# Gates by DMA through DRAM, gate product on GpSimd, activation in PSUM, head reordered, in a recurrence and mixture-of-experts kernel

## Chip, cores and metric

The kernel runs on one core of one Trainium2 chip. The metric is the device time of one execution in microseconds (us), lower is better. Timelines below count from the first instruction of the profiled execution.

## What is computed

A tanh recurrence over 32 time steps gives `h`, with 32 sequences and 128 features. Then `h` is normalised (root mean square), a router picks 4 of 16 experts for each of the 1024 tokens, and all 16 experts are computed densely and summed with their gates, which are zero for those not picked. The result is `x + h + t`.

```python
xw = einsum('ntd,dh->nth', x, Wx) + b
h_t = tanh(xw_t + h_{t-1} @ Wh)                       # 32 steps, h_0 = cond
xn = h * rsqrt(mean(h * h, -1) + 1e-5) * norm_scale
logits = xn @ wg + bg
vals, idx = top_k(logits, 4);  gates = softmax(vals)  # gate_full: (1024, 16)
u = einsum('th,ehd->etd', xn, w1) + b1
a = minimum(u[..., ::2], 7.0);  b = clip(u[..., 1::2], -7.0, 7.0)
s = a * sigmoid(1.702 * a) * (b + 1.0)
y = einsum('eti,eih->eth', s, w2) + b2
out = x + h + einsum('eth,te->th', y, gate_full)
```

All arrays are float32.

## The kernel before

Tokens are laid out in 8 tiles of 128 columns (4 time steps of 32 sequences). Features stand on the partitions, tokens in the free dimension. The engines' programs are written out by hand: each engine runs its own list in order, with semaphores between them.

**Head** (L851 to L893 on TensorE). `keep_warm` issues bf16 matmuls on zeros. Tile 0 of `x` is transposed, `x_wx` multiplies by `Wx`, and `step(t)` (L763) adds `h @ Wh`; ScalarE's `tanh` (L403) makes the next `h`. The head has 8 steps (`HEAD`), with transposes of the other `x` tiles, the transpose of `b1`, sums of squares, `lay_rstd` and fillers between them. Then follow the statistics of the first 2 tiles, `normalise` on VectorE, and the router for them (`route_...`, `gates_...`).

**Unit loop** (L894). A unit is 512 columns wide. There are three stages (`CHUNKS` 2, 2 and 4 tiles): in the first two a unit is two experts by 256 tokens, in the third one expert by 512 tokens; 8, 8 and 16 units, 32 in all (`NU`). For unit `v`:

- TensorE: `up(v, 0)` into psA and `up(v, 1)` into psB (L808), three passes each with rounded high and low parts (float32r); `lay_gates(v - 1)` (L822), which multiplies a selection matrix by the transposed gates `gT`, so that every partition of psG holds the expert's gates; one recurrence step in each of the two slots up to step 31 (`steps_at`); `down(v - LAG)` (L838) in float32, which adds the expert's output to psY. On the way: `sums` and `raw_logits` (at `STATS`), `lay_rstd` (`RSTD`), `transpose_gates` (`GATES_T`), `transpose_out` (`ROWS_OUT`).
- ScalarE: `relu_a` from psA (L458), `swish` from it (L466), the tanh of the steps; before the loop all `w1_high` (L411), which round `w1`.
- VectorE: `lin` from psB (L685), `actg = act * psG` of the unit before (L703), `act` from `lin` and `swish` (L716), the lower parts of `w1` (`w1_low`, L603), `normalise`, and the router's small operations.
- GpSimd: powers (`rstd`, `expo`), `w1_low` for the second half of `w1` (L365), `xn_low`, `place_expo`, and `xh = xT + h` (`add_residuals`).
- SP issues all loads but `wh`, which is on GpSimd's queue, and the stores of each stage's rows.

The bank psM is shared: `psM_turn` fixes an order in which statistics, `rstd`, gates and output transposes take it, each waiting until the one before has been read.

After the last unit: `yT` (L731), four transposes (L937), two copies (L473, L733) and four stores.

## Time and profile before

| | |
|---|---|
| median of 3 runs | 128.18 us (126.57 to 128.47) |
| profiled execution, its time | 127.02 us |
| profiled execution, span from first to last instruction | 124.7 us |
| TensorE busy | 111.3 us, 89% |
| VectorE busy | 89.8 us, 72% |
| ScalarE busy | 65.4 us, 52% |
| GpSimd busy | 24.0 us, 19% |
| mean granted clock of TensorE | 0.999 |

Busy time is a share of the span. Ends of matmuls are modelled and matmuls overlap, so the distance between starts tells more than the lengths. In a timeline row, what stands in brackets is the idle time of the engine before the row and what ended it; `x2` at a float32 matmul counts the two records that one instruction leaves. A row's line number is that of the kernel's source.

### The profile page before, as it was taken

What the parts mean: (1) busy time and instruction counts of PE and PEld (TensorE: products, weight loads), DVE (VectorE), ACT (ScalarE), POOL (GpSimd) and SP (SyncE); (2) the same over time, 40 slices, a digit from 0 to 9 for tenths busy, and PEclk for the clock granted to TensorE, in tenths of its full rate; (3) what the DMA queues carried; (4) which work ended last, traced back from release to release, by engine and by line L of the source; (5) the groups of instructions that cost most, each with busy time, mean ns of one, the idle gap of its engine ahead of it and who ended that gap; (6) DMA issues with size and microseconds to landing.
All of it is one profiled execution on the core that took longest, in us unless ns stands there. A gap on an engine that the chain in (4) does not pass through costs nothing. (4 is left out here: it accounts for less than half of the span.)

```text
span 124.7 us, 1891 instructions
## 1 busy us (share of the span) xinstructions
PE 111.3 (89%) x611; PEld 91.6 (73%) x611; DVE 89.8 (72%) x238; ACT 65.4 (52%) x141; POOL 24.0 (19%) x44
## 2 busy tenths in 40 slices
PE   3669989979999999999999399999999999999850
PEld 2558779969989999899988398877766776677310
DVE  0105659899748999769977779897678877887830
ACT  4014593657663567566756166644665466546210
POOL 5200212940004066206401513000000000000000
PEclk9999999999999999999999999999999999999999
DMA  2899900000000000000000010000001000000003
GB/s 59 178 324 323 334 27 5 0 0 3 0 3 0 5 0 0 0 0 5 0 0 0 3 42 5 0 0 0 0 13 29 0 0 0 8 0 0 0 0 84
DMA packets 6189, 4.52 MB, mean 36 GB/s; under 512 B 754, under 2 KB 6100, under 8 KB 6148
## 3 DMA queue, kind: packets, MB, share of 16 engines
q1 hardware_dynamic: 6148, 4.34, 12.3%
q8 instruction: 5, 0.08, 0.3%
q0 software_dynamic: 32, 0.07, 0.2%
q14 instruction: 4, 0.03, 0.1%
HBM read 3.88 MB, written 0.52 MB: 35 GB/s over the span
## 5 line engine op out<-in xcount | busy, mean ns | idle before, releaser
L458 ACT ACTIVATE relu_a<-psA,lim_b1a 128x256 f32<-128x256 f32 (+1 forms) x48 | 25.8, 546 | 30.4 <-PE psA L808 30.4
L685 DVE TENSOR_SCALAR lin<-psB,one_b1b 128x256 f32<-128x256 f32 (+1 forms) x48 | 26.0, 569 | 16.5 <-PE psB L808 16.2
L838 PE MATMUL psY<-actg,w_sb 128*128 128x256 f32 (+1 forms) x96 | 33.6, 459 | 0.4 <-DVE actg L703 0.3
L808 PE MATMUL psA<-xn_hi,w_hi 128*128 128x256 f32 (+1 forms) x48 | 23.7, 495 | 0.0
L466 ACT ACTIVATE swish<-relu_a,limit_col 128x512 f32<-128x512 f32 x32 | 23.1, 722 | 1.0
L716 DVE SCALAR_TENSOR_TENSOR act<-lin,swish 128x512 f32<-128x512 f32 x32 | 22.3, 695 | 0.0
L703 DVE TENSOR_TENSOR actg<-act,psG 128x512 f32<-128x512 f32 x31 | 21.0, 678 | 0.0
L838 PEld LDWEIGHTS psY<-actg,w_sb 128*128 128x128 f32 x96 | 16.9, 189 | 4.1 <-DVE actg L703 1.9
L808 PE MATMUL psB<-xn_hi,w_hi 128*128 128x256 f32 (+1 forms) x48 | 16.7, 347 | 0.0
L808 PE MATMUL psA<-xn_hi,w_lo 128*128 128x256 f32 (+1 forms) x48 | 15.8, 330 | 0.0
L808 PE MATMUL psA<-xn_lo,w_hi 128*128 128x256 f32 (+1 forms) x48 | 15.8, 330 | 0.0
L808 PE MATMUL psB<-xn_lo,w_hi 128*128 128x256 f32 (+1 forms) x48 | 15.6, 325 | 0.0
L808 PE MATMUL psB<-xn_hi,w_lo 128*128 128x256 f32 (+1 forms) x48 | 15.6, 324 | 0.0
L822 PE MATMUL psG<-gT,select 128*128 128x256 f32 (+1 forms) x47 | 12.4, 320 | 0.8 <-DVE gT L597 0.8
L808 PEld LDWEIGHTS psA<-xn_hi,w_lo 128*128 128x128 f32 x48 | 9.7, 202 | 3.2 <-issue 2.9
L808 PEld LDWEIGHTS psA<-xn_hi,w_hi 128*128 128x128 f32 x48 | 9.6, 201 | 3.2 <-issue 2.9
L763 PEld LDWEIGHTS psR<-hT,wh_sb 128*128 128x128 f32 x56 | 10.0, 218 | 1.1 <-ACT hT L403 0.5
L763 PE MATMUL psR<-hT,wh_sb 128*128 128x32 f32 x56 | 10.1, 265 | 0.3 <-ACT hT L403 0.3
L403 ACT ACTIVATE hT<-psR,b_col 128x32 f32<-128x32 f32 x28 | 7.8, 279 | 4.7 <-PE psR L763 4.5
L808 PEld LDWEIGHTS psA<-xn_lo,w_hi 128*128 128x128 f32 x48 | 9.6, 200 | 0.7
L808 PEld LDWEIGHTS psB<-xn_hi,w_lo 128*128 128x128 f32 x48 | 9.4, 195 | 0.7
L808 PEld LDWEIGHTS psB<-xn_hi,w_hi 128*128 128x128 f32 x48 | 9.4, 195 | 0.7
(105 smaller groups left out, 131.4 us busy)
## 6 DMA issues: line engine op xcount, KB each, us to landing
w_sb<-in_L_ffn_w SPq DMA_DIRECT2D x4, 512.0 KB, 6.7
w_sb<-in_L_ffn_w SPq DMA_DIRECT2D x4, 256.0 KB, 7.2
x_sb<-in_x SPq DMA_DIRECT2D x1, 448.0 KB, 4.7
out<-y_sb SPq DMA_DIRECT2D x8, 32.0 KB, 1.6
out<-y_sb SPq DMA_DIRECT2D x4, 64.0 KB, 1.7
x_sb<-in_x SPq DMA_DIRECT2D x1, 64.0 KB, 2.1
wh_sb<-in_L_cond_Wh POOLq DMA_DIRECT2D x1, 64.0 KB, 2.4
wx_sb<-in_L_cond_Wx SPq DMA_DIRECT2D x1, 64.0 KB, 2.2
```

The costliest lines, as they stand in the source:

```text
L403: nc.scalar.activation(hT[:, (t + 1) * N:(t + 2) * N], step_psum(t), ACT.Tanh, bias=b_col[:, 0:1]).then_inc(step_done, 1)
L458: last = nc.scalar.activation(relu_a[:, u % 2, o], psA[u % 2][:, o], ACT.Relu, scale=-1.0, bias=lim_b1a[:, e0 + k:e0 + k + 1])
L466: nc.scalar.activation(swish[:, u % 3, 0:w], relu_a[:, u % 2, 0:w], ACT.Gelu_apprx_sigmoid, scale=-1.0, bias=limit_col[:, :]).then_inc(swi ...
L685: last = nc.vector.tensor_scalar(lin[:, v % 2, o], psB[v % 2][:, o], one_b1b[:, e0 + k:e0 + k + 1], LIMIT + 1.0, ALU.add, ALU.min)
L703: nc.vector.tensor_tensor(actg[:, u % SUM_DEPTH, o], act[:, u % 2, o], gate_bank(u)[:, o], ALU.mult).then_inc(actg_done, 1)
L716: nc.vector.scalar_tensor_tensor(act[:, v % 2, 0:w], lin[:, v % 2, 0:w], 1.0 - LIMIT, swish[:, v % 3, 0:w], ALU.max, ALU.mult).then_inc(ac ...
L763: nc.tensor.matmul(step_psum(t), wh_sb[:, :], hT[:, t * N:(t + 1) * N], start=False, stop=True, skip_group_check=True).then_inc(step_mm, 1)
L808: last = nc.tensor.matmul(o, w[:, e0 + k, a, :], x_part[:, cols(c)], start=(m == 0), stop=(m == 2))
L822: last = nc.tensor.matmul(gate_bank(u)[:, k * n:(k + 1) * n], select[:, e0 + k, :], gT[:, cols(c)], start=True, stop=True)
L838: last = nc.tensor.matmul(psY[:, 0:n], w2_sb[:, e0 + k, :], actg[:, u % SUM_DEPTH, part(c, k)], start=False, stop=(e0 + k == E - 1))
```

## The change

- `gT` is now 16 rows only. SP writes each pair of tiles' gates to a DRAM scratch (`gate_rows`) and reads it back with a source that repeats for all partitions into `gate_cols`, in four DMAs of four experts each (512 KB a DMA), each with its own semaphore. The matmuls of `lay_gates`, the selection matrix and the split of the gates into high and low parts go.
- The product `actg = act * gates` moves from VectorE to GpSimd (`gate_product`), two units behind; the last unit's stays on VectorE. `LAG` goes from 2 to 4, `act` has 6 buffers.
- ScalarE's relu and swish write in place to psA; `act` reads it there. psA is now free when `act` is done, not when relu is.
- `b2` is used as it is, in float32; `round_b2` goes.
- Bank psG becomes psX, which holds late `x` tiles, the gate transposes and the output transposes, in an order of its own. The last stage sums in psR.
- `add_residuals` writes to `xT` in place.
- Head: 6 fillers of 512 columns instead of 9 of 128, then fillers of 256 columns at all steps; `x` in three loads (4, 12 and 16 time steps), the last behind the first quarter of `w1`; `wh` from SP, `b` and `norm_scale` from ScalarE's queue; all of `w1` ahead of `w2`. Tiles 6 and 7 of `x` are transposed in unit 0.
- ScalarE does 10 of the 16 `w1_high` before the loop and two in each of units 0 to 2. GpSimd takes the second half of all pairs of `w1_low`; VectorE's `w1_low(1)` comes after the first router operations.

The diff, cut:

```diff
-    WARM, WARM_START = 128, 9
-    LAG = 2
-    SUM_DEPTH = 5
+    WARM, WARM_START, WARM_GAP = 512, 6, 256
+    LAG = 4
+    POOL_LAG = 2
+    ACT_DEPTH, SUM_DEPTH = 6, 5
 
...
-    RSTD, GATES, GATES_T = [[None] + [v + k for v in STATS[1:]] for k in (1, 3, 4)]
-    ROWS_OUT = [UNIT0[c + 1] + LAG + 3 for c in range(NC - 1)] + [None]
+    RSTD = [None] + [v + 1 for v in STATS[1:]]
+    GATES, GATES_T = [[k] + [v + 3 + k for v in STATS[1:]] for k in (0, 1)]
+    ROWS_OUT = [UNIT0[c + 1] + LAG + 2 for c in range(NC - 1)] + [None]
+
+    GATE_HALF = [2, 0, 1, 2]
+    GATE_GROUPS = 4
+    EQ = E // GATE_GROUPS
...
+        def y_bank(c):
+
+            return psR if c == NC - 1 else psY
...
+        def gate_block(u, o):
+
+            c, e0, r = unit(u)
+            k = GATE_HALF[first_pair(c)] * PW
+            n = CHUNKS[c] * P
+            if r > 1:
+                return gate_cols[:, e0:e0 + r, k:k + n]
+            return gate_cols[:, e0, k + o.start:k + o.stop]
+
+        def gates_here(eng, u):
+
+            c, e0, r = unit(u)
+            for q in range(first_pair(c), first_pair(c + 1)):
+                for k in range(e0 // EQ, (e0 + r - 1) // EQ + 1):
+                    eng.wait_ge(cols_loaded[q][k], 16)
...
-            sp.dma_start(rows[N:N + 1, :], b.rearrange("(a n) -> a n", a=1)).then_inc(rows_loaded, 16)
-            sp.dma_start(rows[N + 1:N + 2, :], norm_scale.rearrange("(a n) -> a n", a=1)).then_inc(rows_loaded, 16)
-            sp.dma_start(x_sb[:, TL:T, :], x[:, TL:T, :]).then_inc(x_loaded, 16)
+            sp.dma_start(wh_sb[:, :], wh).then_inc(wh_loaded, 16)
+            sp.dma_start(x_sb[:, TL:4 * TL, :], x[:, TL:4 * TL, :]).then_inc(x1_loaded, 16)
             sp.dma_start(wg_sb[:, :], wg).then_inc(wg_loaded, 16)
             for g in range(NG):
                 ge = slice(g * EG, (g + 1) * EG)
...
                     sp.dma_start(b1_sb[:, :], b1).then_inc(b1_loaded, 16)
+                    sp.dma_start(x_sb[:, 4 * TL:T, :], x[:, 4 * TL:T, :]).then_inc(x_loaded, 16)
...
+            sp.dma_start(b2_sb[:, :], b2).then_inc(b2_loaded, 16)
+
+            def spread_gates(q):
+
+                qc = slice(q * PW, (q + 1) * PW)
+                sp.wait_ge(x_read, psX_turn(("gates", q)))
+                sp.dma_start(gate_rows[:, qc], gT[:, qc]).then_inc(rows_written, 16)
+                sp.wait_ge(rows_written, 16 * (q + 1))
+                if GATE_HALF[q] in GATE_HALF[:q]:
+                    sp.wait_ge(actg_done, UNIT0[1])
+                for k in range(GATE_GROUPS):
+                    es = slice(k * EQ, (k + 1) * EQ)
+                    sp.dma_start(gate_cols[:, es, gate_slice(q)],
+                                 gate_rows[es, qc].partition_broadcast(P)).then_inc(cols_loaded[q][k], 16)
+
...
+            for q in range(3):
+                spread_gates(q)
+            sp.wait_ge(x_read, psX_turn(("out", 0)))
+            store_rows(0)
+            spread_gates(3)
+            sp.wait_ge(x_read, psX_turn(("out", 1)))
+            store_rows(1)
+            sp.wait_ge(rows_ready, 2)
+            store_rows(2)
...
-            pool.dma_start(wh_sb[:, :], wh).then_inc(wh_loaded, 16)
...
-                pool.wait_ge(xT_ready, 3)
-                nc.gpsimd.tensor_tensor(xh[:, qc], xT[:, qc], hT[:, N + q * PW:N + (q + 1) * PW],
+                pool.wait_ge(x_read, psX_turn("x"))
+                nc.gpsimd.tensor_tensor(xT[:, qc], xT[:, qc], hT[:, N + q * PW:N + (q + 1) * PW],
...
+            def gate_product(u):
+
+                pool.wait_ge(act_done, u + 1)
+                gates_here(pool, u)
+                if u >= SUM_DEPTH:
+                    pool.wait_ge(y_mm, u - SUM_DEPTH + 1)
+                w = slice(0, width(u))
+                r = unit(u)[2]
+                nc.gpsimd.tensor_tensor(actg[:, u % SUM_DEPTH, w].rearrange("p (r n) -> p r n", r=r),
+                                        act[:, u % ACT_DEPTH, w].rearrange("p (r n) -> p r n", r=r),
+                                        gate_block(u, w).rearrange("p (r n) -> p r n", r=r) if r == 1
+                                        else gate_block(u, w), ALU.mult).then_inc(actg_done, 1)
+
+            w1_low(0)
             power_rstd(0)
+            w1_low(1)
             power_rstd(1)
+            w1_low(2)
             power_expo(0)
             place_expo(0)
...
-                    w1_low(v + 3)
+                if v + W1_LOW_AHEAD < NP:
...
-                for q in at(GATES, v):
-                    if q == 1:
-                        add_residuals(0)
+                if v >= POOL_LAG:
+                    gate_product(v - POOL_LAG)
+                for q in at(GATES, v - 1):
                     add_residuals(q)
...
+            acte.dma_start(rows[N:N + 1, :], b.rearrange("(a n) -> a n", a=1)).then_inc(rows_loaded, 16)
+            acte.dma_start(rows[N + 1:N + 2, :], norm_scale.rearrange("(a n) -> a n", a=1)).then_inc(rows_loaded, 16)
...
-            for k in range(HEAD - W1_AT - 2, 2 * NP):
+            for k in range(HEAD - W1_AT - 2, 2 * W1_AHEAD):
...
-                    last = nc.scalar.activation(relu_a[:, u % 2, o], psA[u % 2][:, o], ACT.Relu, scale=-1.0,
+                    last = nc.scalar.activation(psA[u % 2][:, o], psA[u % 2][:, o], ACT.Relu, scale=-1.0,
                                                 bias=lim_b1a[:, e0 + k:e0 + k + 1])
...
-                nc.scalar.activation(swish[:, u % 3, 0:w], relu_a[:, u % 2, 0:w], ACT.Gelu_apprx_sigmoid, scale=-1.0,
...
+                if u + W1_AHEAD < NP:
+                    w1_high(2 * (u + W1_AHEAD))
+                    w1_high(2 * (u + W1_AHEAD) + 1)
...
-                mark(nc.vector.tensor_tensor(
+                nc.vector.tensor_tensor(
                     gates[:, ts, :], gate_sum[:, ts, :],
-                    inv[:, ts].rearrange("p (j o) -> p j o", o=1).to_broadcast([P, 2, E]), ALU.mult))
-
...
+                    inv[:, ts].rearrange("p (j o) -> p j o", o=1).to_broadcast([P, 2, E]),
+                    ALU.mult).then_inc(scale_done, 1)
...
             dve.wait_ge(x_t, 1)
             nc.vector.tensor_copy(xT[:, 0:P], psB[0][:, 0:P]).then_inc(xT_ready, 1)
+            dve.wait_ge(x_t, 2)
+            nc.vector.tensor_copy(xT[:, P:2 * P], psB[0][:, P:2 * P]).then_inc(xT_ready, 1)
             dve.wait_ge(m_read, psM_turn("rows"))
...
-            dve.wait_ge(x_t, 2)
-            nc.vector.tensor_copy(xT[:, P:4 * P], psB[1][:, 0:3 * P]).then_inc(xT_ready, 1)
-
...
+            stats(0)
+            dve.wait_ge(x_t, 3)
+            nc.vector.tensor_copy(xT[:, 2 * P:4 * P], psB[1][:, 0:2 * P]).then_inc(xT_ready, 1)
             w1_low(0)
...
+            normalise(1)
...
-            normalise(1)
...
-            w1_low(2)
-            dve.wait_ge(x_t, 3)
...
+            w1_low(1)
...
-                if 1 <= v <= NU:
-                    u = v - 1
-                    dve.wait_ge(g_mm, u + 1)
-                    dve.wait_ge(act_done, u + 1)
-                    if u >= SUM_DEPTH:
-                        dve.wait_ge(y_mm, u - SUM_DEPTH + 1)
-                    for o in pieces(u):
-                        nc.vector.tensor_tensor(actg[:, u % SUM_DEPTH, o], act[:, u % 2, o], gate_bank(u)[:, o],
-                                                ALU.mult).then_inc(actg_done, 1)
...
+                    if v >= ACT_DEPTH:
+                        dve.wait_ge(actg_done, v - ACT_DEPTH + 1)
                     w = width(v)
-                    nc.vector.scalar_tensor_tensor(act[:, v % 2, 0:w], lin[:, v % 2, 0:w], 1.0 - LIMIT,
-                                                   swish[:, v % 3, 0:w], ALU.max, ALU.mult).then_inc(act_done, 1)
-                if v + 3 < NP:
-                    w1_low(v + 3)
+                    nc.vector.scalar_tensor_tensor(act[:, v % ACT_DEPTH, 0:w], lin[:, v % 2, 0:w], 1.0 - LIMIT,
+                                                   psA[v % 2][:, 0:w], ALU.max, ALU.mult).then_inc(act_done, 1)
                 if v == 0:
-                    copy_gates(0)
+                    dve.wait_ge(x_mm, psX_turn("x"))
+                    nc.vector.tensor_copy(xT[:, 4 * P:NT * P], psX[:, 0:(NT - 4) * P]).then_inc(x_read, 1)
+                    w1_low(2)
+                if v + W1_LOW_AHEAD < NP:
+                    w1_low(v + W1_LOW_AHEAD)
                 for q in at(RSTD, v):
                     route_index(q)
                 for q in at(GATES, v):
                     gates_scale(q)
-                    gates_high(q)
+            u = NU - 1
+            dve.wait_ge(act_done, NU)
+            gates_here(dve, u)
+            dve.wait_ge(y_mm, u - SUM_DEPTH + 1)
+            for o in pieces(u):
+                nc.vector.tensor_tensor(actg[:, u % SUM_DEPTH, o], act[:, u % ACT_DEPTH, o], gate_block(u, o),
+                                        ALU.mult).then_inc(actg_tail, 1)
...
-            def keep_warm(n):
+            def keep_warm(n, w=WARM_GAP):
...
+            def turn_x(what):
+
+                if psX_turn(what) > 1:
+                    pe.wait_ge(x_read, psX_turn(what) - 1)
...
             def transpose_gates(q):
-                pe.wait_ge(parts_ready, q + 1)
-                turn(("gates", q))
+                pe.wait_ge(scale_done, q + 1)
+                turn_x(("gates", q))
...
+                    last = nc.tensor.transpose(psX[0:E, k * P:(k + 1) * P], gates[:, j, :], ident[:, :])
+                last.then_inc(x_mm, 1)
...
-            def lay_gates(u):
-
-                c, e0, r = unit(u)
-                n = CHUNKS[c] * P
...
-                for k in range(r):
-                    last = nc.tensor.matmul(gate_bank(u)[:, k * n:(k + 1) * n], select[:, e0 + k, :], gT[:, cols(c)],
-                                            start=True, stop=True)
-                last.then_inc(g_mm, 1)
...
             def down(u):
                 c, e0, r = unit(u)
                 n = CHUNKS[c] * P
+                bank = y_bank(c)
                 if u == UNIT0[c]:
-                    if c:
+                    if c == 0:
+                        pe.wait_ge(b2_loaded, 16)
+                    elif c < NC - 1:
                         pe.wait_ge(yT_ready, c)
-                    nc.tensor.matmul(psY[:, 0:n], b2_rows[:, :], gT[:, cols(c)], start=True, stop=False)
-
-                pe.wait_ge(actg_done, u + len(pieces(u)))
+                    pe.wait_ge(x_read, psX_turn(("gates", first_pair(c + 1) - 1)))
+                    nc.tensor.matmul(bank[:, 0:n], b2_sb[:, :], gT[:, cols(c)], start=True, stop=False)
+
+                if u < NU - 1:
+                    pe.wait_ge(actg_done, u + 1)
+                else:
+                    pe.wait_ge(actg_tail, len(pieces(u)))
...
             def transpose_out(c):
                 pe.wait_ge(yT_ready, c + 1)
-                turn(("out", c))
+                turn_x(("out", c))
                 for k in range(CHUNKS[c]):
                     j = TILE0[c] + k
-                    last = nc.tensor.transpose(psM[:, k * P:(k + 1) * P], yT[:, j * P:(j + 1) * P], ident[:, :])
-                last.then_inc(m_mm, 1)
+                    last = nc.tensor.transpose(psX[:, k * P:(k + 1) * P], yT[:, j * P:(j + 1) * P], ident[:, :])
+                last.then_inc(x_mm, 1)
...
-            keep_warm(WARM_START)
+            keep_warm(WARM_START, WARM)
...
+            keep_warm(1)
...
                 step(t)
-
                 if t == 0:
-                    pe.wait_ge(x_loaded, 16)
-                if t < 3:
-                    last = transpose_x(t + 1, psB[1], t)
-                if t == 2:
-                    last.then_inc(x_t, 1)
-                if t == 3:
+                    keep_warm(3)
+                elif t == 1:
+                    pe.wait_ge(x1_loaded, 16)
+                    transpose_x(1, psB[0], 1).then_inc(x_t, 1)
+                elif t == 2:
+                    transpose_x(2, psB[1], 0)
+                    keep_warm(1)
+                elif t == 3:
                     x_wx(1, 1)
-                if t == 4:
+                    keep_warm(1)
+                elif t == TL:
                     pe.wait_ge(b1_loaded, 16)
                     turn("b1")
                     for a in range(2):
                         last = nc.tensor.transpose(psM[:, a * E:(a + 1) * E], b1_sb[:, a::2], ident[0:E, 0:E])
                     last.then_inc(m_mm, 1)
-                if t == TL + 1:
+                    keep_warm(2)
+                elif t == TL + 1:
                     pe.wait_ge(consts_ready, 1)
                     sums(0).then_inc(m_mm, 1)
-                if 3 <= t < HEAD - 1:
+                    keep_warm(2)
+                elif t == TL + 2:
+                    transpose_x(3, psB[1], 1).then_inc(x_t, 1)
                     keep_warm(1)
-                if t == HEAD - 1:
+                else:
                     lay_rstd(0)
+                    keep_warm(2)
...
-            for j in range(4, NT):
-                if j == X_SPLIT:
-                    lay_rstd(1)
-                last = transpose_x(j, psG, j - 4)
-            last.then_inc(x_t, 1)
+            pe.wait_ge(x_loaded, 16)
+            transpose_x(4, psX, 0)
+            lay_rstd(1)
             x_wx(2, XW_TILES - 2)
+            transpose_x(5, psX, 1)
```

## Rows read from the trace of the kernel before

**Rows 1.** The page: span, and each engine's busy time, share and instructions
```profile
span 124.7 us, 1891 instructions
...
PE 111.3 (89%) x611; PEld 91.6 (73%) x611; DVE 89.8 (72%) x238; ACT 65.4 (52%) x141; POOL 24.0 (19%) x44
```

**Rows 2.** Timeline, a period of the last stage: start us, length, engine, line, operation
```profile
101.08 0.80 PE L808 MATMUL psA<-xn_hi,w_hi 128*128 128x512 f32 x1
...
101.85 0.69 DVE L716 SCALAR_TENSOR_TENSOR act<-lin,swish 128x512 f32<-128x512 f32 x1
...
102.87 0.39 PE L822 MATMUL psG<-gT,select 128*128 128x512 f32 x1
...
103.10 1.02 PE L838 MATMUL psY<-actg,w_sb 128*128 128x512 f32 x2
...
103.56 0.80 PE L808 MATMUL psA<-xn_hi,w_hi 128*128 128x512 f32 x1
```

**Rows 3.** Timeline, first stage, units 3 and 4: first matmul of each
```profile
31.12 0.47 PE L808 MATMUL psA<-xn_hi,w_hi 128*128 128x256 f32 x1
...
34.11 0.47 PE L808 MATMUL psA<-xn_hi,w_hi 128*128 128x256 f32 x1
```

**Rows 4.** Timeline, the longest wait of TensorE in the unit loop
```profile
70.62 0.41 PE L847 MATMUL psM<-ident,yT 128*128 128x128 f32 x2 [2.14 <-DVE xn L506]
```

**Rows 5.** Timeline of the head and of the clock's rise
```profile
7.46 0.63 PE L747 MATMUL psB<-ident,x_sb 32*128 32x32 f32 x4 [1.22 <-DMA x_sb<-in_x]
...
10.00 0.42 ACT L411 ACTIVATE w_hi<-w_sb 128x256 fp32r<-128x256 f32 x1
...
14.67 0.64 PE L763 MATMUL psR<-hT,wh_sb 128*128 128x32 f32 x2 [0.27 <-ACT hT L403]
...
15.34 0.29 ACT L403 ACTIVATE hT<-psR,b_col 128x32 f32<-128x32 f32 x1 [0.40 <-PE psR L763]
...
18.06 0.22 DVE L610 CAST b_hi<-b_sb 16x128 fp32r<-16x128 f32 x1 [0.30 <-DMA b_sb<-in_L_ffn_b]
...
19.09 0.35 DVE L506 SCALAR_TENSOR_TENSOR xn<-hT,b_col,psM 128x128 f32<-128x128 f32 x1
...
20.51 0.78 PE L808 MATMUL psA<-xn_hi,w_hi 128*128 128x256 f32 x1
...
21.72 0.41 PE L808 MATMUL psA<-xn_hi,w_lo 128*128 128x256 f32 x1
...
26.41 0.28 PE L808 MATMUL psB<-xn_hi,w_lo 128*128 128x256 f32 x1
...
26.53 0.28 PE L808 MATMUL psB<-xn_lo,w_hi 128*128 128x256 f32 x1
```

**Rows 6.** Timeline, two pieces of GpSimd work
```profile
24.23 2.15 POOL L365 TENSOR_TENSOR w_lo<-w_sb,w_hi 128x256 fp32r<-128x256 f32 x3
...
47.49 1.42 POOL L372 TENSOR_TENSOR xh<-xT,hT 128x256 f32<-128x256 f32 x2
```

**Rows 7.** Timeline, two VectorE operations beside that work
```profile
25.84 1.09 DVE L716 SCALAR_TENSOR_TENSOR act<-lin,swish 128x512 f32<-128x512 f32 x1
...
48.10 0.68 DVE L703 TENSOR_TENSOR actg<-act,psG 128x512 f32<-128x512 f32 x1
```

**Rows 8.** Windows: stretch, length, busy PE, PEld, DVE, ACT, POOL, clock, DMA share, GB/s
```profile
12.00:15.00 3.00, 2.73 (x15) 2.36 (x15) 1.81 (x8) 1.70 (x6) 0.81 (x1) 1.00 1.11 365
30.00:35.00 5.00, 5.00 (x38) 4.79 (x37) 4.23 (x9) 3.38 (x9) 0.00 (x0) 1.00 0.00 0
45.00:55.00 10.00, 10.00 (x77) 9.49 (x76) 7.98 (x25) 6.55 (x18) 3.58 (x6) 1.00 0.00 0
```

**Rows 9.** The page: a DMA issue, out<-in, queue, count, size, us to landing
```profile
out<-y_sb SPq DMA_DIRECT2D x8, 32.0 KB, 1.6
```

**Rows 10.** Timeline, the tail of the unit loop
```profile
115.27 0.39 PE L822 MATMUL psG<-gT,select 128*128 128x512 f32 x1
...
119.47 0.75 DVE L731 TENSOR_TENSOR yT<-xh,psY 128x256 f32<-128x256 f32 x2 [1.22 <-PE psY L838]
```

189 lines of the change are left out of this document (65 added, 124 removed).

## The prediction

> **What bounds the kernel now.** The page of the profile comes first: span 124.7 us, TensorE busy 111.3 us of it, VectorE 89.8, ScalarE 65.4, GpSimd 24.0 [rows 1]. A busy TensorE need not be a full one, so the timeline of one period of the last stage is read next: one unit's first matmul starts at 101.08, the next unit's at 103.56, so a unit takes 2.48 us [rows 2]. In it stand six `up` matmuls of 512 columns, one gate matmul and one fp32 `down` (two records). The gate matmul's slot is 102.87 to 103.10, 0.23 us [rows 2]; seven such slots are 1.62, which leaves 0.86 for `down`. 7 x 0.232 + 0.86 = 2.48: TensorE has no gap, it sets the pace. In the first stage a unit takes 34.11 - 31.12 = 2.99 us [rows 3]. A 256-column slot is 26.53 - 26.41 = 0.12 us [rows 5]: twelve `up` and two gate slots are 1.67, two `down` 0.86, two recurrence steps the remaining 0.46. So TensorE's own work sets the pace of the unit loop, except for stalls such as the 2.14 us at 70.62, where the output transpose waited for `normalise` because both use bank psM [rows 4].
>
> The head is different. The granted clock reads 1.00 everywhere, yet the same 256-column matmul takes 0.41 us at 21.72 and 0.28 at 26.41 [rows 5]; slot and length show the lower of the two levels (1.2 GHz) until about 25.3 and the upper (2.4 GHz) afterwards, and the rise came after TensorE had worked without a break from about 20. The head's chain is: transposes wait 1.22 us for `x` (7.46), step 1 stands behind their 0.56 us, the last head step starts at 14.67, and the first `up` at 20.51 [rows 5].
>
> **Stretch 1, up to the first `up`: 20.5 becomes 15.4.** TensorE was free at 7.46 - 1.22 = 6.24 [rows 5]. The second load of `x` is now cut to three tiles (192 of 448 KB), no weights stand in front, and its wait stands behind step 1. So step 1 starts about 6.5, not 8.0. The two one-row loads go to ScalarE's queue, `wh` to SP's: each delays only what needs it later (the table load, ready long before the first tanh). From step 1 to step 7 it is now 6.65 us. A step costs 0.67 from its start to the tanh (14.67 to 15.34), then 0.29 for the tanh [rows 5], 1.01 with the handover. At the upper level the step before the tanh is about 0.35, and ScalarE's 0.29 + 0.42 (`w1_high`) [rows 5] limits the step to about 0.75; six of them and a late rise give 4.9: step 7 at 11.4. At the lower level the wider fillers (two of 256 columns, 0.43) make each step 1.2 and step 7 comes at 13.6. From step 7 to the first `up` it is 5.84 us; the four `b2` operations before `normalise(1)` (18.06 to 19.09 [rows 5], 1.0 us) go, as do most transposes of late `x` tiles; 4.0 stays at the upper level, 5.3 at the lower. First `up` between 15.4 and 18.9. I take 15.4: six 512-column fillers at the start and fillers in every step leave TensorE few gaps, which is nearer to what it did before 25.3 than to the old head.
>
> **Stretch 2, to the start of unit 4: 13.6 becomes 12.3.** Before, 34.11 - 20.51 = 13.6 us [rows 3, 5], lower level for its first 5 us, with two `down` units in it. Now LAG is 4, so no `down` stands here, but other things do. ScalarE had 3.38 us busy in 5 us [rows 8], 2.0 per unit of 2.99; it gains two `w1_high` (0.84) in units 0 to 2, so 2.9 and handovers, 3.1: it bounds the stage, since each step waits for a tanh queued behind these. The `x` transposes add about 0.8 to TensorE. Worst is the wait in `transpose_gates(0)` at the end of unit 1: VectorE does `gates_sum`, `act(0)`, the xT copy, two `w1_low` and only then `gates_scale`, about 6.9 us after the first `up`, while TensorE would arrive at 5.2. Unit 2's `up`, its steps and all behind them queue there. 2.9 + 4.3 + 2.5 + 2.6 = 12.3.
>
> **Stretch 3, unit 4 to the last `down`: 85.3 becomes 78.9.** Before, from 34.11 to about 119.4, where VectorE takes over at 119.47 [rows 3, 10]. Gate matmuls of 29 units go: 13 x 0.236 + 16 x 0.232 = -6.8. The stall of 2.14 goes, as the output transposes move to psX: -2.1. `b2` becomes fp32, four passes for one: two of 256 columns and one of 512, 2 x 0.31 + 0.63 = +1.25. Two more `down` units are carried over: +1.75. In the tail 115.27 to 119.4 is 4.2 us [rows 10] for work of 2 x 0.23 + 3 x 0.86 = 3.0; with four `down` queued TensorE doesn't wait there: -1.1. Small waits at unit 4: +0.6. The end after it, 124.7 - 119.4 = 5.3, is unchanged.
>
> **What must hide.** (a) The gate product moves to GpSimd, whose trace has no 512-column product. Two 256-column sums took 1.42 us [rows 6], so 0.71 each: 512 columns cost between 0.71 and 1.42; I take 1.4. Other GpSimd work is 3.58 us in 10 [rows 8], 1.1 per unit; 2.5 against a unit of 2.76 in the first stage, 1.4 against 2.25 in the last. It fits; without that cover each product costs its excess over the unit. (b) VectorE and GpSimd can hold each other up: `act` with both inputs in SBUF took 1.09 us at 25.84 while GpSimd's `w1_low` ran until 26.38, against 0.69 at 101.85; the product with an input in PSUM took 0.68 at 48.10 while GpSimd ran from 47.49 [rows 2, 6, 7]. In the new kernel `act` reads one input from PSUM, so it is like the second. The Trainium skill (GPSIMD Engine Reference, Key points) says that contention comes with VectorE instructions in a 2-port mode or with two SBUF inputs; the trace agrees. Against the change speaks the same page's Engine selection, which sends elementwise products to VectorE; its 2.6 cycles per element at 1.2 GHz would make the product an estimated 1.1 us and leave the sum as it is, and no run here shows the 512-column form yet. (c) The gates travel 16 x 256 values to DRAM and back to 128 partitions, 2 MB for each of four pairs of tiles. A 32 KB store took 1.6 us [rows 9], the load rate was 365 GB/s [rows 8]: write 1.6, first of four reads 1.6 + 1.4, the others 1.4 each. gT(0) is copied at 7.7 after the first `up`, first gates at 12.3, product(0) at 13.7; `down(0)` comes at about 16.4. At half the rate the first product comes at 15.2, still in time. For the last stage pair 3 is spread from unit 17: 4.6 us, or 2.1 units, and `down(16)` comes in unit 20. SP issues these in order, with the row stores between; nothing else waits in that queue. (d) relu and swish in place in PSUM: psA is now free at `act`, some 3.0 us after the unit starts, and needed after 2 x 2.25 = 4.5. ScalarE writing PSUM isn't in the trace; bounds 0 and +0.3 per pass, hidden by its 48% idle share either way.
>
> **Sum.** 15.4 + 12.3 + 78.9 + 5.3 = 111.9 us of span against 124.7, so -12.8. The profiled execution took 127.02 us; the median of the runs is 128.18. 128.2 - 12.8 = 115.4, taken as 115.5.
>
> **Rivals.**
> 1. The clock stays at the lower level through the head, or falls back in stretch 2 with its waits. First `up` 18.9, and some 2 us more at half speed after it: +5.5, so 121. For it: the old head had fillers in most steps, and the level rose only after continuous work. Against: those were 128 columns, one a step; the new ones put about 0.43 us beside a step of 0.64. The 2.14 us stall did not lower it.
> 2. Gates or products come late: the first `down` of each stage waits 1 to 2 us, and GpSimd runs beside a VectorE that holds it up for `act` (0.69). 1.4 + 0.69 + 1.1 = 3.2 against 2.76 in twelve units: +5, 120.5. Against: the 0.68 at 48.10.
> 3. Slower: GpSimd is the bound at 2.5 us or more a product. The stages cost (2.5 + 1.1 - 2.76) x 14 = 11.8 and (2.5 - 2.25) x 16 = 4: 131. It decides above 2.3 us, where the loss passes the 12.8 gained. For it: nothing in rows beyond 1.42; a broadcast load filling SBUF at the same time is not in the trace.
> 4. The gain in the head is eaten by ScalarE and VectorE in stretch 2 and by the later `down`s, and a stall replaces the one at 70.62: about 126.
>
> **Chances.** Forecast 0.55 (113 to 118), rival 1 0.2, rival 2 0.14, rival 4 0.06, rival 3 0.05. The range 112 to 122.5 takes in rivals 1 and 2. About 2% is what a measurement of this kernel can tell from no change: faster 0.91, within 2% 0.04, slower 0.05.
>
> **What would show it.** Right: period of the last stage 2.25; first `up` at 15 to 16 with slots of 0.12 at once; product 1.2 to 1.4 us; VectorE's `act` at 0.69 beside it; TensorE waiting at `transpose_gates(0)`. Wrong: slots of 0.21 after the first `up` (rival 1); TensorE's loader waiting for the product in mid-stage (2, 3); `down(0)`, `down(8)` or `down(16)` behind a DMA.

## The result, and the profile after

The changed kernel is slower. Its median is 132.91 us of 4 runs (131.14 to 133.72) beside 128.32 us of the kernel before on the same chip (126.57 to 128.49): a ratio of 1.039, interval 1.024 to 1.054. The forecast was 115.5 us, range 112 to 122.5. The profiled execution took 133.0 us, span 131.2 against 124.7 [rows 1].

Executions of one kernel here differ by 1 to 2.6 us, in good part by where TensorE's clock falls in the head; smaller differences are read below from traces that have the same level there.

First the page of the changed kernel: the busy times, four of the rows in 40 slices (each slice 3.3 us), the product's group, and the reads of the gates (count, size, median us to landing).

```profile
span 131.2 us, 1767 instructions
PE 111.9 (85%) x572; PEld 86.5 (66%) x572; DVE 74.7 (57%) x186; ACT 62.9 (48%) x142; POOL 60.9 (46%) x71
...
PE   6899999789999999999998999200499999999960
...
PEclk9965555799999999999999999965558999999998
DMA  1898940005649200669716999629994100000003
GB/s 48 223 230 266 291 124 0 0 8 144 159 126 165 48 5 5 148 123 175 145 61 125 133 149 145 137 79 144 130 153 131 34 10 0 0 0 0 0 0 80
...
L425 POOL TENSOR_TENSOR actg<-act,gate_cols 128x512 f32<-128x512 f32 x31 | 39.3, 1279 | 35.1 <-DMA gate_cols<-gate_rows 24.0
...
gate_cols<-gate_rows SPq DMA_DIRECT2D x16, 512.0 KB, 10.4
```

VectorE is down from 89.8 to 74.7 us and GpSimd up from 24.0 to 60.9 [rows 1], as meant. But TensorE has four nearly empty slices (82 to 95 us), and after them the clock is at its lower level. The bottom rows say why: while gates are read, the DMA engines move only about 125 to 175 GB/s, whether their mean share is 4 to 6 tenths (first group of slices) or 9 (later ones). The weight loads before had 365 GB/s [rows 8], and this kernel's own early slices reach 291. A read of 512 KB takes 10.4 us to land.

The chain that ended last, around the gap (start us, length, what):

```profile
63.33 4.94 DMA gate_rows<-gT
69.79 2.13 SPq L333
71.96 1.84 SPq L339
73.85 1.71 SPq L339
75.60 1.56 SPq L339
77.21 1.38 SPq L339
78.64 7.36 DMA gate_rows<-gT
86.01 5.96 DMA gate_cols<-gate_rows
92.20 1.27 POOL actg L425
93.51 2.07 PE psR L851 x2
```

It goes through SyncE and the DMA, not through an engine that computes. Pair 2's write (63.33) already took 4.94 us to land, while pair 1's reads were still running. Pair 3's gates were copied to SBUF by ScalarE at 73.52. SyncE stood at the stores of stage 1's rows (L339), each of which took it 1.4 to 1.8 us to issue while pair 2's reads were running. The 16 KB write of pair 3 (78.64) landed 7.4 us later, behind the same reads; the first of its own reads took 6 us more. The first `down` of the last stage:

```profile
81.59 1.12 PE L842 MATMUL psR<-gT,b_sb 16*128 16x512 f32 x2
93.51 2.07 PE L851 MATMUL psR<-actg,w_sb 128*128 128x512 f32 x2 [10.80 <-POOL actg L425]
94.59 1.42 PE L829 MATMUL psA<-xn_hi,w_hi 128*128 128x512 f32 x1
95.81 0.63 PE L829 MATMUL psA<-xn_hi,w_lo 128*128 128x512 f32 x1
```

TensorE waited 10.80 us, and then ran 512-column matmuls at 0.63 us (slots of 0.43) instead of 0.39 (0.23): the granted clock had gone to 0.50 during the break (at about 86 us) and came back at about 99.6.

The rest of the loop is what was forecast. One period of the last stage, to be held against [rows 2]:

```profile
106.22 0.79 PE L829 MATMUL psA<-xn_hi,w_hi 128*128 128x512 f32 x1
...
106.75 0.69 DVE L722 SCALAR_TENSOR_TENSOR act<-lin,psA 128x512 f32<-128x512 f32 x1
...
107.52 1.28 POOL L425 TENSOR_TENSOR actg<-act,gate_cols 128x512 f32<-128x512 f32 x1 [0.97 <-DVE act L722]
...
108.47 0.79 PE L829 MATMUL psA<-xn_hi,w_hi 128*128 128x512 f32 x1
```

A unit takes 2.25 us where it took 2.48.

And the head: the step behind the first, the first `up`, and the windows around the fall of the clock (columns as in [rows 8]).

```profile
6.06 0.41 PE L780 MATMUL psY<-hT,wh_sb 128*128 128x32 f32 x2
...
17.77 0.58 PE L829 MATMUL psA<-xn_hi,w_hi 128*128 128x256 f32 x1
18.15 0.41 PE L829 MATMUL psA<-xn_hi,w_lo 128*128 128x256 f32 x1
```

```profile
6.00:9.00 3.00, 2.92 (x19) 2.27 (x19) 0.43 (x2) 1.25 (x6) 0.00 (x0) 0.75 1.00 242
9.00:12.00 3.00, 3.00 (x17) 2.71 (x17) 0.41 (x3) 1.43 (x6) 1.30 (x2) 0.50 0.80 244
```

The upper level was there from about 4 us (the step at 6.06 takes 0.41 us, those of the old head 0.64) and was lost near 7.5, although TensorE was busy 2.92 of 3.00 us; it came back near 24.5. The first `up` starts at 17.77 instead of 20.51 [rows 5].

### The profile page after: what moved, and what is told of

It is laid out like the page before. It is cut to its first block, busy times and chain, and to the rows that moved or that the text cites. A ratio compares the mean times of both kernels' runs of the same rounds, so it can differ in the third digit from the quotient of the medians.

```text
span 131.2 us, 1767 instructions
## 1 busy us (share of the span) xinstructions
PE 111.9 (85%) x572; PEld 86.5 (66%) x572; DVE 74.7 (57%) x186; ACT 62.9 (48%) x142; POOL 60.9 (46%) x71
## 4 chain that ended last, share of the span: by engine, by line
PE 61%; DMA 14%; DVE 10%; SPq 8%; issue 2%; POOL 1%; ACT 1%; POOLq 0%; ACTq 0%
PE psB L829 13%; PE psA L829 13%; PE psR L851 12%; DMA gate_rows<-gT 9%; SPq L339 5%; DMA gate_cols<-gate_rows 5%; PE psY L851 5%; PE psR L780 3%; PE psA L809 3%; SPq L333 3%; PE psR L772 2%; DVE lin L698 2%; PE psM L787 2%; PE psX L761 2%; DVE act L722 1%
## 5 line engine op out<-in xcount | busy, mean ns | idle before, releaser
L425 POOL TENSOR_TENSOR actg<-act,gate_cols 128x512 f32<-128x512 f32 x31 | 39.3, 1279 | 35.1 <-DMA gate_cols<-gate_rows 24.0
L515 ACT ACTIVATE psA<-psA,lim_b1a 128x256 f32<-128x256 f32 (+1 forms) x48 | 24.6, 518 | 42.6 <-PE psA L829 42.6
L851 PE MATMUL psR<-actg,w_sb 128*128 128x512 f32 x32 | 17.6, 653 | 10.8 <-POOL actg L425 10.8
L722 DVE SCALAR_TENSOR_TENSOR act<-lin,psA 128x512 f32<-128x512 f32 x32 | 21.9, 684 | 1.1 <-DVE lin L698 0.4
L521 ACT ACTIVATE psA<-psA,limit_col 128x512 f32<-128x512 f32 x32 | 21.2, 662 | 1.0
L851 PE MATMUL psY<-actg,w_sb 128*128 128x256 f32 x64 | 17.3, 393 | 0.0
L829 PE MATMUL psB<-xn_hi,w_hi 128*128 128x256 f32 (+1 forms) x48 | 17.2, 358 | 0.0
L851 PEld LDWEIGHTS psR<-actg,w_sb 128*128 128x128 f32 x32 | 6.5, 206 | 14.6 <-POOL actg L425 11.6
L851 PEld LDWEIGHTS psY<-actg,w_sb 128*128 128x128 f32 x64 | 11.2, 190 | 2.0 <-POOL actg L425 0.4
L780 PE MATMUL psR<-hT,wh_sb 128*128 128x32 f32 x56 | 10.6, 274 | 0.0
## 6 DMA issues: line engine op xcount, KB each, us to landing
gate_cols<-gate_rows SPq DMA_DIRECT2D x16, 512.0 KB, 10.4
```

The lines of the kernel that those rows point to most:

```text
L425: nc.gpsimd.tensor_tensor(actg[:, u % SUM_DEPTH, w].rearrange("p (r n) -> p r n", r=r), act[:, u % ACT_DEPTH, w].rearrange("p (r n) -> p r ...
L515: last = nc.scalar.activation(psA[u % 2][:, o], psA[u % 2][:, o], ACT.Relu, scale=-1.0, bias=lim_b1a[:, e0 + k:e0 + k + 1])
L521: nc.scalar.activation(psA[u % 2][:, 0:w], psA[u % 2][:, 0:w], ACT.Gelu_apprx_sigmoid, scale=-1.0, bias=limit_col[:, :]).then_inc(swish_do ...
L722: nc.vector.scalar_tensor_tensor(act[:, v % ACT_DEPTH, 0:w], lin[:, v % 2, 0:w], 1.0 - LIMIT, psA[v % 2][:, 0:w], ALU.max, ALU.mult).then_ ...
L780: nc.tensor.matmul(step_psum(t), wh_sb[:, :], hT[:, t * N:(t + 1) * N], start=False, stop=True, skip_group_check=True).then_inc(step_mm, 1)
L829: last = nc.tensor.matmul(o, w[:, e0 + k, a, :], x_part[:, cols(c)], start=(m == 0), stop=(m == 2))
```

## The experiments

**Theory A**: the only thing that makes the kernel slower is the rate at which gates are read back from DRAM; without it the changed kernel would take 119.5 us. It had two forms at first, A1 (many partitions reading the same row is slow) and A2 (1 KB pieces are slow by themselves). Rivals are given with each run. "Before" is always the kernel before on the same chip.

### Without the transport

e1_preloaded: no gates are spread; the products read weights laid down once, so the output isn't that of the reference.

```
-            for q in range(3):
-                spread_gates(q)
+            for k in range(GATE_GROUPS):
+                ... sp.dma_start(gate_cols[:, es, q * PW:(q + 1) * PW], w1_v[:, es, :]) ...
```

> The changed kernel without its gate transport: no row goes to DRAM, the products read 4 MB of rows of w1 that were loaded once behind w2, so the gates are not the router's. Theory A (the late gates of pair 3 are the loss): TensorE's 11.3 us wait before down(16) and the 2 to 3 us at the lower clock level behind it go, nothing else changes: span 131.2 - 13.5 = 117 to 118, 119.5 us of time, 7% under the kernel before. Rival B (the loss is in the head and in GpSimd's product, and the wait would appear elsewhere): span above 124.

Measured: 119.69 us (119.65 to 119.73, 4 runs), ratio to before 0.933, interval 0.931 to 0.935; span 117.9. The transport costs 13.2 us, and everything else in the change is worth 8.5 us. Theory A held; its 119.5 us are still 4 us above the 115.5 of the prediction. The traced run had its first `up` at 18.81, the changed kernel's at 17.77; the four runs lie within 0.1 us.

### What makes the reads slow

e2_distinct: the same DMAs and sizes, but each partition reads rows of w1 of its own, one behind the other; the products use these and not the gates.

```
-                                 gate_rows[es, qc].partition_broadcast(P)).then_inc(cols_loaded[q][k], 16)
+                                 w1_v[:, es, :]).then_inc(cols_loaded[q][k], 16)
```

> Same DMAs at the same places with the same sizes and 1 KB pieces, but each partition reads a row of its own (of w1) instead of all 128 reading the same row; the gates are therefore not the router's. Theory A1 (the repeated source row is slow): the reads of 512 KB move at 300 GB/s or more instead of 145, the wait before down(16) shrinks from 11.3 to under 2 us, span about 118. Rival A2 (1 KB pieces into SBUF beside a busy kernel are slow, whatever their source): the rate stays at 130 to 170 GB/s and the span at 131.

Measured: 119.67 us, landing median 6.1 us, 266 to 347 GB/s in the slices that are nearly full. The 1 KB piece is not slow by itself: A2 fell.

e3_long: scratch and SBUF laid out so that a partition's four experts are one piece of 4 KB. e3_copies: the same with 16 copies in DRAM, eight partitions reading each.

```
+        gate_rows = nc.dram_tensor("gate_rows", [R, NQ, E, PW], F32)      # R = 1; 16 in e3_copies
+        gate_cols = sb("gate_cols", [P, 3, E, 2 * P])
```

> The source still repeats for all partitions, but the scratch and gate_cols are laid out so that a partition's four experts of a DMA are one piece of 4 KB instead of four of 1 KB; results are the reference's. A1 (repeated source): the rate stays near 145 GB/s, span 129 to 132. A2 (small pieces): the rate doubles, span about 118.

> As the one with 4 KB pieces, and the scratch holds 16 copies of the rows, each read by 8 partitions only; the write to DRAM grows from 16 KB to 256 KB. A1: readers of one row fall from 128 to 8, the rate rises to 250 to 350 GB/s, the wait before down(16) falls under 3 us, span 118 to 121. If the rate stays at 145 as well, the number of readers per row is not the cause and A1 falls.

Measured for e3_long: 119.66 us, landing 5.6 us, up to 409 GB/s, although all 128 partitions still read the same rows. A1, as I had put it, fell: that many read one row is not enough. Measured for e3_copies: 129.38 us (128.86 to 132.75, 7 runs), ratio 1.008, interval 1.004 to 1.013. That missed as well. SyncE's queue in it:

```profile
28.82 0.35 SPq L329 DMA_DIRECT2D gate_rows<-gT  x1
32.89 2.52 SPq L337 DMA_DIRECT2D gate_cols<-gate_rows  x4
```

The write is now 256 KB and lands after 4.1 us, where 16 KB take 1.4; reads take 8.0 us to land, mostly at 221 to 253 GB/s. A remedy against a cause that wasn't there brought delays of its own: the first product came at 39.14 (34.59 in the changed kernel), TensorE waited 2.6 us there already, and 5.2 us ahead of the last stage. The 16 copies lie 64 KB apart in DRAM; whether that spacing made these reads slower than those of e3_long (8.0 against 5.6 us) was not tested.

e3_long had changed two things, the size of a piece and the spacing of the rows in DRAM (1 KB from row to row instead of 4 KB). The next runs take them apart. In e5_packed pieces stay 1 KB and only the scratch is packed; in e6_two_kb it is packed too and pieces are 2 KB.

```
-        gate_rows = nc.dram_tensor("gate_rows", [E, NT * P], F32)
+        gate_rows = nc.dram_tensor("gate_rows", [NQ, E, PW], F32)
...
-                sp.dma_start(gate_rows[:, qc], gT[:, qc]).then_inc(rows_written, 16)
+                sp.dma_start(gate_rows[q, :, :], gT[:, qc]).then_inc(rows_written, 16)
...
-                                 gate_rows[es, qc].partition_broadcast(P)).then_inc(cols_loaded[q][k], 16)
+                                 gate_rows[q, es, :].partition_broadcast(P)).then_inc(cols_loaded[q][k], 16)
```

> Against the changed kernel only the layout of the DRAM scratch changes: the 16 gate rows of a pair lie one behind the other (1 KB apart) instead of 4 KB apart. The destination in SBUF stays as it was, so the pieces stay 1 KB, and all 128 partitions still read the same rows. It splits what the run with 4 KB pieces had changed together. Theory P (size of a piece: many partitions reading one row are slow when the pieces are 1 KB): landing median near 10 us, rate 125 to 175 GB/s, a stall of 8 to 11 us ahead of stage 3, time 130 to 134 us. Rival S (spacing of the source rows: 4 KB apart falls on the same part of the memory): landing median 5.5 to 6.5 us, rate over 260 GB/s, no stall, time 119.5 to 120 us.

> Source packed as in the run with 4 KB pieces, all partitions reading the same rows, but the destination in SBUF is laid out by pairs of experts, so that the pieces are 2 KB. Theory P (size of a piece): the rate lies between those of 1 KB (about 145 GB/s) and 4 KB (300 to 409 GB/s) pieces, say 200 to 290 GB/s, landing median 6 to 8.5 us; the reads of a pair (2 MB) then take 7 to 10 us and are in time or nearly: 119.6 to 123 us. Rival S (spacing of the source rows): as with 4 KB pieces, over 300 GB/s, landing median 5.6, 119.7 us.

Measured: 118.73 us and 118.66 us, landing 6.1 and 5.8 us. Size hardly matters (6.1, 5.8, 5.6 us for 1, 2 and 4 KB), the spacing decides: theory P fell, S held (its time, 119.5 to 120, was 0.8 us too long; the traces of both runs have the upper level at the start of the head). The page and the queue of e5_packed, whose only difference to the changed kernel is three lines of addresses:

```profile
PE   5999999978999999999999989999999999999940
...
GB/s 43 171 254 227 352 257 23 0 0 8 152 367 200 0 0 6 0 15 294 361 61 6 151 314 293 19 272 303 139 0 32 16 0 0 0 0 0 0 0 90
...
gate_cols<-gate_rows SPq DMA_DIRECT2D x16, 512.0 KB, 6.1
```

```profile
64.30 2.01 SPq L333 DMA_DIRECT2D gate_cols<-gate_rows  x4
67.88 1.97 SPq L339 DMA_DIRECT2D out<-y_sb  x4
73.46 0.32 SPq L327 DMA_DIRECT2D gate_rows<-gT  x1
74.89 2.59 SPq L333 DMA_DIRECT2D gate_cols<-gate_rows  x4
```

The four stores are issued in 1.97 us instead of 6.6, the write of pair 3 goes out 0.4 us after its copy (73.06) and lands in 1.4. Windows of four us while reads run, the changed kernel first, then e5_packed (last two columns: DMA share, GB/s):

```profile
72.00:76.00 4.00, 4.00 (x20) 3.17 (x19) 3.44 (x6) 2.70 (x5) 4.00 (x4) 1.00 1.08 135
```

```profile
68.00:72.00 4.00, 3.61 (x20) 2.80 (x19) 3.93 (x10) 2.22 (x5) 3.71 (x5) 1.00 1.07 347
```

In these two windows the DMA engines are as full, and they move 2.6 times as much in the second. The share is not what tells the slow reads, though: the changed kernel's first reads run at 126 to 159 GB/s with a share of 4 to 6 tenths (the page above, 30 to 39 us).

Is it a gap between rows, or a gap of 4 KB? e8_pitch5 and e8_pitch16 put 5 and 16 KB from row to row.

```
-        gate_rows = nc.dram_tensor("gate_rows", [NQ, E, PW], F32)
+        gate_rows = nc.dram_tensor("gate_rows", [NQ, E, 1280], F32)      # 4096 in e8_pitch16
```

> As the kernel with the packed scratch (rows of 1 KB one behind the other, landing median 6.1 us, 118.73 us), but with 5 KB from one gate row to the next in DRAM: 4 KB of unused space between them. Pieces 1 KB, the same rows for all partitions, 2 MB a pair. Theory C (a spacing of exactly 4 KB puts all 16 rows on the same part of the memory): 5 KB shifts each row by 1 KB, so the reads are fast again, landing median 6 to 6.5 us, no stall ahead of stage 3, 118.5 to 119.9 us. Rival G (any gap between the rows is slow, since the four rows of one read no longer lie together): landing median near 10 us, 125 to 175 GB/s, 130 to 134 us as with 4 KB.

> As before, with 16 KB from one gate row to the next. Theory C (rows at multiples of 4 KB fall on the same part of the memory): at least as slow as at 4 KB, landing median 10 us or more, 130 us or more; if the part chosen hangs on higher address bits too, slower still (20 us, over 140). Rival G (any gap is slow, and the same for all gaps): the same 10 us as 4 KB and as 5 KB. Rival W (only 4 KB itself): 6 us and 119 us.

Measured: 119.67 us at 5 KB (landing 5.9 us), and 157.65 us at 16 KB, the longest of all, with TensorE waiting 28.5 us ahead of the last stage. The page of e8_pitch16:

```profile
DMA  2889400155578916659922355453554682000002
GB/s 75 238 225 324 133 0 0 30 84 84 88 85 85 76 26 84 85 85 81 153 59 66 88 84 89 86 84 82 76 82 88 91 153 83 0 0 0 0 0 67
...
gate_cols<-gate_rows SPq DMA_DIRECT2D x16, 512.0 KB, 16.7
```

At 16 KB the rate stays at about 85 GB/s while the DMA engines' share goes up and down between about 3 and 9 tenths. So theory C held in these two runs: rows 1, 4, 16 KB apart are read at up to 367, about 145 and about 85 GB/s, and 5 KB apart at up to 363. The Trainium skill (DMA: Bandwidth & Descriptors, section "Latency and other measured facts") has an entry that large powers of two between the rows in HBM cost rate, and that a few KiB of padding bring it back. It speaks of 512 KiB and more between the partitions' rows. The runs agree with the kind of the rule and carry it down to 4 and 16 KB, for rows that all partitions share.

e11_distinct4 asks whether the spacing alone does it: each read takes 512 different rows of w1, all 4 KB apart (the products use them in place of the gates).

```
-                                 gate_rows[es, qc].partition_broadcast(P)).then_inc(cols_loaded[q][k], 16)
+                                 w1.rearrange("(a b) h i -> a (b h) i", b=4)
+                                 .rearrange("a (p s) i -> p s a i", s=4)[:, 0, :, :]
+                                 ).then_inc(cols_loaded[q][k], 16)
```

> The changed kernel, but each read of gates takes 512 different 1 KB rows of w1 that lie 4 KB apart, one for each partition and expert, instead of four rows of the scratch for all partitions; the product therefore multiplies by values of w1 and not by the gates. Writes, queue, pieces, destination and bytes stay. Theory C (only where the addresses lie decides: multiples of 4 KB are slow): landing median near 10 us, 125 to 175 GB/s, a stall ahead of stage 3, 129 to 134 us. Rival D (it takes both: a wide spacing and 128 partitions that read the same few rows): landing near 6 us, 119 to 120 us. The earlier run with different rows had read w1 without gaps, so it did not tell these apart.

Measured: 119.7 us, landing 5.2 us. C in its strict form fell, D held: it takes both, a spacing of 4 KB or 16 KB and few rows (four a read here) that all partitions ask for. Few rows and many readers of one row were not taken apart. What in the memory the rows share at that spacing was not shown by any run; 512 different rows 4 KB apart cover 2 MB and can differ in ways in which four rows do not.

### The order in SyncE's queue

e4_order: slow reads as in the changed kernel, but pair 3 is spread ahead of the stores of stage 1's rows.

```
-            for q in range(3):
+            for q in range(4):
                 spread_gates(q)
             sp.wait_ge(x_read, psX_turn(("out", 0)))
             store_rows(0)
-            spread_gates(3)
```

> Only the order in SyncE's queue changes: pair 3's gates are written and read back ahead of the four stores of stage 1's rows instead of behind them. Reads stay 1 KB pieces from one DRAM row for all partitions, rows 4 KB apart. Theory A (the slow rate of the reads is the cause, the order only adds to it): in the changed kernel pair 3's write was issued at 78.64 us and had landed at 86.01, its gates having lain ready since 73.5 us; now the write is issued near 73.6, still lands behind pair 2's reads (near 82), the first product of stage 3 runs near 88 instead of 92.2, and the time is 127 to 130 us. Rival O (the order is the cause by itself): the stall before stage 3 is under 1 us and the time 119 to 121 us. Rival N (the order is hidden behind the reads anyway): 131 to 133 us.

Measured: 130.52 us in a single run, between theory A's 127 to 130 and rival N's 131 to 133; before on that chip had 126.74. Its queue:

```profile
75.32 0.32 SPq L327 DMA_DIRECT2D gate_rows<-gT  x1
84.86 3.00 SPq L333 DMA_DIRECT2D gate_cols<-gate_rows  x4
87.91 14.31 SPq L339 DMA_DIRECT2D out<-y_sb  x8
```

The write goes out 3.3 us earlier than in the changed kernel but then needs 9.5 us instead of 7.4, since it still stands behind pair 2's reads. The reads start only 1.2 us earlier (2.4, if the 1.25 us are taken off by which this trace is late from its head on). The first product of the last stage came at 91.07 (expected near 88, 92.20 in the changed kernel), and TensorE waited 8.24 us for it instead of 10.80. Rival O fell, and the order is worth about 2.5 us of that wait, by two traces; whether the time gains as much, one run can't tell. The rate is the cause.

### A version that beats both

e7_long_again times the version with 4 KB pieces in rounds, e10_packed_timed the one with nothing but a packed scratch.

> The kernel with 4 KB pieces (scratch and SBUF laid out so that four experts' gates of a pair are one contiguous piece for a partition; nothing else changed) measured in rounds against the kernel before, since it is the version that should beat both. One look gave 119.66 us. Theory A (the transport at full rate costs nothing on the path): 119.5 to 119.9 us, a ratio to the kernel before of 0.93, as without any transport of gates (119.69 us). Rival: its reads come within a few us of being late and in other runs they are: a median of 121 us or more, or runs that scatter by over 1 us.

> The changed kernel with nothing but the scratch packed (1 KB from row to row), measured in rounds, since one look only has stood behind it so far (118.73 us). It beats both kernels by either reading: 118.2 to 119.8 us, ratio to the kernel before 0.92 to 0.945. If the height of the time hangs on where the level falls in the head, the runs lie near 118.4 and near 119.7 and nowhere else, as those with 4 KB pieces did.

Measured: 119.02 us (118.23 to 120.61, 6 runs), ratio 0.933, interval 0.923 to 0.943; and 119.16 us (118.48 to 119.72, 4 runs), ratio 0.937, interval 0.924 to 0.950. Packed, the change gains 6 to 7%. For e7_long_again theory A had 119.5 to 119.9, which the median missed by 0.5 us, and the runs scatter by 2.4 us, which was the rival's sign; but the reads are in time in its trace (no wait of TensorE for a product), and its runs near 118.3 have a mean granted clock of 0.92 as e5_packed has, those near 119.7 one of 0.99 or 1.00. The scatter is laid to the level in the head; that is argued for the runs without a trace. The packed kernel's runs lie at 118.48, 118.62, 119.71 and 119.72. Two traces show the two heights, 118.73 us with the level falling at about 8 us and the first `up` at 17.82, and 119.71 us with slots of the lower level all through the head and the first `up` at 18.80. The other traces bear this out: the profiled runs of e1_preloaded, e2_distinct, e3_long, e7_long_again, e8_pitch5, e11_distinct4 and this one all have their first `up` at 18.80 or 18.81 and took 119.66 to 119.73 us. At the same level, then, a packed transport costs nothing over none at all.

### The clock in the head

On the packed kernel, the fillers between the head's steps are 512 or 128 columns wide instead of 256.

```
-    WARM, WARM_START, WARM_GAP = 512, 6, 256
+    WARM, WARM_START, WARM_GAP = 512, 6, 512      # 128 in e9_fill128
```

> Packed scratch, and the fillers between the steps of the head 512 columns wide instead of 256 (0.21 us each at the upper level, 0.43 at the lower). With 256 columns the granted clock fell to 0.50 at about 7.7 us and rose again near 24.8; first up at 17.8. Theory H (wider fillers hold TensorE at the upper level, as the prediction took for 256): granted clock 1.00 and steps of 0.75 to 1.0 us, first up at 15.5 to 16.5, span 114.5 to 115.7, time 116 to 118. Rival L (the fall doesn't hang on the fillers): the level falls near 7.7 all the same, each wider filler costs 0.21 us in a head bound by TensorE, steps of 1.6 us, first up at 19.5 to 20.5, time 120 to 121.5.

> Packed scratch, the same fillers 128 columns wide. Theory H: less work, so the level falls no later than at 256 columns (7.7 us) and probably earlier, near 4 to 5 us; steps get shorter by 0.1 us for each filler, which gives back about 1.0 us: first up at 17 to 18.3, time 118 to 119.2. Rival L (fillers only cost at the lower level): as H at first, but the level falls at the same 7.7 and first up comes at 16.8, time 117.7. Rival K (fillers shorten the time at the lower level at its end, near 24.8): the level rises 2 us or more later and the time is over 120.

> Packed scratch and fillers of 512 columns in the head, in rounds. Theory H (wider fillers hold the upper level longer, to 14 us instead of 7.7, which is worth 1.0 us): 117.5 to 118.2 us, 0.5 to 2 us below the packed kernel with 256 columns on the same chip. Rival: that run was a lucky one, and the median is that of the packed kernel within 0.4 us.

Measured: 117.88 us with 512 columns, 120.43 with 128. The two don't compare as they stand: the trace of e9_fill128 has the lower level from its first steps (0.64 us each), that of e9_fill512 the upper. Against e10_packed_timed, which has the lower level too, e9_fill128 had its first `up` 0.2 us earlier (18.62) but its clock rose only at about 30.7 instead of 26 us: rival K's late rise and its time of over 120. Two windows of e9_fill512, and its first `up`:

```profile
9.00:12.00 3.00, 2.64 (x20) 2.28 (x22) 0.60 (x4) 2.12 (x8) 1.31 (x2) 1.00 0.79 238
12.00:15.00 3.00, 2.64 (x18) 1.77 (x17) 2.06 (x8) 2.15 (x8) 2.30 (x3) 0.93 1.01 327
```

```profile
15.96 0.58 PE L829 MATMUL psA<-xn_hi,w_hi 128*128 128x256 f32 x1
```

The upper level held until about 14.6 us and the first `up` came at 15.96, 1.9 us earlier than with 256 (17.82); unit 4 starts only 0.9 us earlier (30.42, not 31.31), as the clock rose later, at about 28.1 us instead of 25. But in rounds the same kernel has 114.52, 116.45, 122.35 and 122.47 us: the median, 119.4, is no gain. The trace of the 122.35 us run has slots of the lower level from the start, steps of about 1.5 us and the first `up` at 20.57. Theory H holds for the one traced run that begins at the upper level, where with wider fillers it held to 14.6 us instead of about 8; in a run that doesn't, each filler costs twice (a slot of 0.43 us instead of 0.21). Neither "a lucky run" nor "1 us" is right: wide fillers widen the spread at both ends.

e12_scale_first has 512-column fillers and moves one small VectorE operation up; e13_scale_256 does so with 256-column fillers; e14_scale_512_again is e12_scale_first on the chip of e13_scale_256.

```
                 if v == 0:
                     ... (copy of xT)
+                    gates_scale(0)
                     w1_low(2)
                 if v + W1_LOW_AHEAD < NP:
                     w1_low(v + W1_LOW_AHEAD)
...
-                for q in at(GATES, v):
-                    gates_scale(q)
+                for q in at(GATES, v):
+                    if q:
+                        gates_scale(q)
```

> Packed scratch, fillers of 512 columns, and on VectorE gates_scale(0) ahead of two w1_low (0.3 to 0.5 us each) instead of behind them. TensorE waits 0.8 to 1.4 us for it at the end of unit 1. Theory W (that wait is on the path, as the prediction had it): it falls to under 0.4 us, the first read of gates is issued as much earlier, and the time falls by 0.5 to 1.0 us, to 116.8 to 117.4. Rival S (ScalarE bounds that stretch, and TensorE waits for a tanh instead): the wait goes, the start of unit 4 stays within 0.2 us, and so does the time.

> Packed scratch, fillers of 256 columns as in the changed kernel, and gates_scale(0) ahead of the two w1_low on VectorE. With 512-column fillers and the lower level from the start, that move took 1.9 us off the span (120.6 to 118.7), because TensorE's break at the end of unit 1 had also put off the rise of the clock from 27.3 to 32.6 us. Theory W: here the level had risen before that break (24.8 us), so only the wait itself goes, 0.8 to 1.1 us: start of unit 4 near 31.3 instead of 32.3, runs near 117.6 and 118.7 where the packed kernel has 118.5 and 119.7. Rival S (something else queues there when the level is already up: ScalarE's tanh): 118.3 to 119.7 as before.

> The kernel with 512-column fillers and gates_scale(0) first once more, on the same chip as the one with 256, because its four runs lay between 112.68 and 121.08 us. Theory B (which level the head gets differs from run to run, and wide fillers raise both ends): runs near 112.7 to 116 where the upper level holds and near 120.5 where it doesn't, a spread of over 3 us, against under 2 us with 256 columns. Rival: the spread was that chip's, and both kernels lie within 1.5 us here.

Measured: e12_scale_first 112.68, 120.47, 120.52 and 121.08 us (median 120.5); e13_scale_256 118.63 us (117.66 to 119.45, 6 runs), ratio 0.926, interval 0.918 to 0.933; e14_scale_512_again 115.22 and five runs from 120.22 to 121.00. The traces of e10_fill_timed and of e12_scale_first have the same level in the head, so they show what the move does. First without it, then with it:

```profile
29.54 0.60 PE L820 MATMUL psX<-ident,gates 128*16 128x128 f32 x2 [0.81 <-DVE gates L634]
...
32.28 0.41 PE L829 MATMUL psB<-xn_hi,w_hi 128*128 128x256 f32 x1
...
32.71 0.29 PE L829 MATMUL psB<-xn_lo,w_hi 128*128 128x256 f32 x1
...
34.94 0.36 PE L829 MATMUL psA<-xn_hi,w_hi 128*128 128x256 f32 x1
```

```profile
27.21 0.38 PE L831 MATMUL psB<-xn_hi,w_lo 128*128 128x256 f32 x1
27.42 0.28 PE L831 MATMUL psB<-xn_lo,w_hi 128*128 128x256 f32 x1
...
28.03 0.38 PE L822 MATMUL psX<-ident,gates 128*16 128x128 f32 x2
...
32.83 0.36 PE L831 MATMUL psA<-xn_hi,w_hi 128*128 128x256 f32 x1
```

The wait of 0.81 us is gone, but unit 4 starts 2.1 us earlier (32.83, not 34.94): matmuls reach 0.28 us at 27.4 instead of 32.7. With a break of 0.8 us just ahead of it, the rise came 5 us later. The trace of e14_scale_512_again repeats it (no wait, rise at about 27.8, unit 4 at 32.81), and in e9_fill512 and e9_fill128, where the same 0.81 us also stand ahead of the rise, it came late too (28.1 and 30.7 us). The expected 116.8 to 117.4 us were missed, since these runs begin at the lower level. With 256 columns the traced run (118.99 us) starts unit 4 at 31.55 where the packed one at the same level has 32.28, 0.73 us, just under theory W's 0.8 to 1.1. The medians, from two chips, differ by 0.5 us, which is less than a kernel's own spread; taken by the two heights, runs lie at 117.66 to 118.27 and 118.99 to 119.45 where the packed kernel's lie at 118.48 to 118.62 and at 119.7. Theory B held: 5.8 us between the runs with 512 columns, 1.8 with 256. The version to keep is e13_scale_256, or e10_packed_timed if simplicity counts: the step between them rests on traces, not on medians.

## Why the prediction was wrong

The step that failed is (c) of what must hide: the way of the gates through DRAM, put at 365 GB/s or at worst half of it, and at 4.6 us for pair 3, hidden under TensorE's work. It ran at about 145 GB/s, pair 3's first product came 18.7 us after its gates had been copied, and that cost 13.8 us in the last stage.

**Stretch 1 (20.5 to 15.4).** Measured 17.77. The chain was right: step 1 at 6.06 (forecast 6.5), no wait for x, no `b2` operations. The choice between the ends was wrong. I took the upper end because the fillers "leave TensorE few gaps"; the level fell near 7.5 us with TensorE busy 2.92 of 3.00. From 17.77, 15.4 was 2.4 us off and 18.9, my lower-level figure, 1.1. In the packed kernel's span of 116.9 us (e5_packed), against 111.9 in the sum, that reading is still the largest piece. Two runs, 114.52 and 112.68 us with wider fillers, got as far as the forecast or past it (the second with `gates_scale(0)` moved up as well); that the upper level held through their heads is argued from their time and a mean granted clock of 0.989 and 0.996, as they have no trace.

**Stretch 2 (13.6 to 12.3).** Measured 13.46 (17.77 to 31.23). The named wait was there, 1.36 us in `transpose_gates(0)`, but half of the stretch, up to about 24.5 us, ran at the lower level, and the sum had taken the upper. By e12_scale_first's trace this wait costs more than its length where it stands ahead of the rise.

**Stretch 3 (85.3 to 78.9): the step that failed.** Measured 94.71 (31.23 to 125.94). The packed kernel has 80.38 (31.31 to 111.69), so the terms for TensorE were 1.5 us short; 0.6 of it is `b2`, whose slot is 0.63 us for 256 columns and 1.05 for 512, 0.2 over that of a `down` in each of three places. The rest of it was not followed. The other 14.3 us are the gates. The last group of `down` starts at 121.49 instead of 107.24; of that 0.44 had come before the wait, 10.87 are the wait, and 2.95 the lower level behind it (from the first to the fourth `down` 10.01 us instead of 7.06).

**What must hide.** (a) The product takes 1.28 us, between the forecast of 1.4 and the estimate of 1.1 and inside the period of 2.25. (b) All 32 `act` take 0.67 to 0.69 us, with GpSimd busy for 60.9 us of the span; no contention, as the row with an input in PSUM had said. (d) relu and swish in place in PSUM take 0.66 us; nothing waits for them.

(c) is where it went wrong, in two terms. The first is the rate. "At half the rate the first product comes at 15.2, still in time": it started at 34.59 and ended at 35.86, 18.1 us after the first `up`, later than the 16.4 at which `down(0)` had been put. It was in time all the same, barely and by luck: with the lower level in the head TensorE reached `down(0)` only at 35.92. The rate measured was 145 GB/s, 0.4 of the row it was taken from, below even my lower bound: a load in which each partition reads its own rows is not the nearest row for one in which all read the same four, 4 KB apart. And I put the bound to pair 0 only. The gates of pairs 2 and 3 are ready 10.6 us apart (62.93 and 73.52); 2.1 MB in that time are 198 GB/s, which the full rate has nearly twice over and half of it, 182, has not.

The second is "4.6 us" for pair 3 with "nothing else waits in that queue". From the copy of its gates at 73.52 to the first product it took 18.7 us: 5.1 behind the stores, whose issue stood behind pair 2's reads, 7.4 for the write behind the same reads, 6.2 until its own first read had landed. In the packed kernel it takes 6.3 us (73.06 to 79.31), and the product ends 1.6 us before `down(16)` wants it at 82.20.

**The rivals.** Rival 1 (clock in the head) happened at 2.4 us in stretch 1 and at most 1.2 in stretch 2, of its 5.5. Rival 2 had the right place (the first `down` of a stage) for 1 to 2 us and the wrong engine: GpSimd's 1.28 us never bound. Rival 3 came near the right time, 131 us, by luck, from a product of 2.5 us where it took 1.28; by its own sum it also decides above 2.4 us and not 2.3. No rival had the transfer itself as the bound, though the trace had no row of its kind. The list of signs was better than the rivals: it ends with "`down(16)` behind a DMA", and that is what the profile shows. The transfer should have been the slower rival, with 198 GB/s as the point from which it decides.

**The last line of the sum.** It took 12.8 us off the median of the kernel before, whose time lies 2.3 us above the span in the profiled execution. In the changed kernel and its packed form that distance is 1.8 us (133.0 and 131.2; 118.73 and 116.9), so a span of 111.9 us would have been a time of about 113.7. The forecast of 115.5 had 1.8 us in hand that no term accounts for.

## What to carry to other kernels

When gates, scales or any small table goes through DRAM to reach all partitions, pack its rows or pad them (5 KB from row to row did it here): with 4 KB from row to row this kernel took 14 us more than packed and with 16 KB 39 us more, a difference of three lines of addresses. Before you cost such a transfer from a load of weights, ask what is different in its addresses, and compute for every consumer the rate at which it would be late, not only for the first. And look at what shares its queue: a slow transfer holds up the stores and tiny writes behind it as well.

## What was not expected of the hardware

- Four 1 KB rows read by 128 partitions: at most 367 GB/s with 1 KB from row to row, about 145 with 4 KB, about 85 with 16 KB, at most 363 with 5 KB. 512 different rows 4 KB apart: at most 352. The mean share of the DMA engines doesn't tell these apart: at 16 KB the rate was 84 GB/s at a share of 0.95 (69 to 73 us) and 89 at 0.50 (93 to 97 us).
- What a DMA's issue takes depends on the transfers ahead of it: four 32 KB stores took SyncE 6.63 us to issue behind slow reads, 1.97 behind fast ones, 11.80 behind the slowest.
- A granted clock of 1.00 in the rows of the head does not mean the upper level: the traces of 118.73 and 119.71 us differ in that the first shows a fall to 0.50 and the second shows 1.00 throughout, with 256-column slots of 0.21 us, those of the lower level. The slots decide.
- With a break of 0.81 us in TensorE's work ahead of the rise of the clock, the rise came at 32.6 us, without it at 27.3 and 27.8; in the break of 10.80 us in the changed kernel the level fell, and the lower one lasted until about 99.6 us (granted clock 0.59 from 98 to 100 us).
